# A selective-scan recurrence on one NeuronCore: outputs summed turned in PSUM, one of four input scalings on VectorE

## The reference

```python
u, res = silu(x @ W_in[:, :256]), (x @ W_in[:, 256:])
delta  = softplus(u @ W_delta + b_delta)          # 512 positions x 256 channels
Bm, Cm = u @ W_B, u @ W_C                         # 512 positions x 16 states
# over time, for each of 256 channels and 16 states:
h[t] = exp(delta[t] * A) * h[t-1] + delta[t] * B[t] * u[t]
y[t] = sum over the 16 states of h[t] * C[t]
out  = ((y + u * D_param) * silu(res)) @ W_out
```

## Time and profile before

| | us |
|---|---|
| median of 3 runs (lowest, highest) | 1144.26 (1143.19, 1144.58) |
| the profiled execution: its own time | 1145.62 |
| its span, first to last instruction | 1143.8 |
| TensorE busy in the span | 837.0 (73%) |
| VectorE busy | 816.1 (71%) |
| ScalarE busy | 700.0 (61%) |
| GpSimd busy | 292.4 (26%) |

### The profile page before, as it was taken

The page is one execution under the profiler, slowest core; times in us unless marked ns, Lnnn a source line. Parts: engine busy times, 40 slices in busy tenths (PEclk is TensorE's granted clock), DMA queues, the critical chain, the costliest instruction groups (busy, mean ns, idle before and its releaser), DMA issues. The chain is left out here.

```text
span 1143.8 us, 12084 instructions
## 1 busy us (share of the span) xinstructions
PE 837.0 (73%) x3574; PEld 505.8 (44%) x3576; DVE 816.1 (71%) x1651; ACT 700.0 (61%) x2225; POOL 292.4 (26%) x170
## 2 busy tenths in 40 slices
PE   2661285999977489998976137699996847998883
PEld 2450244555746334354445023455574633435432
DVE  2169745887555679998976873688845568999993
ACT  1411449995478385956851235999458828596591
POOL 0002103886356300000001110488635520000000
PEclk9865586999999899999996559699999979999997
DMA  8101002321000000000000001132100000000000
GB/s 229 38 0 33 0 8 61 93 93 47 1 1 1 1 1 1 0 1 0 1 19 0 0 1 37 42 96 95 32 1 1 1 0 1 1 1 1 1 1 19
DMA packets 26812, 27.37 MB, mean 24 GB/s; under 512 B 7172, under 2 KB 17146, under 8 KB 26746
## 3 DMA queue, kind: packets, MB, share of 16 engines
q1 hardware_dynamic: 24776, 24.63, 7.4%
q10 hardware_dynamic: 1970, 1.97, 0.6%
HBM read 25.28 MB, written 1.31 MB: 23 GB/s over the span
## 5 line engine op out<-in xcount | busy, mean ns | idle before, releaser
L1553 POOL TENSOR_TENSOR rs<-ve,minus_half 128x4 f32<-128x4 f32 (+1 forms) x56 | 89.3, 1596 | 647.6 <-DVE ve L1194 558.4
L943 PE MATMUL ps<-mem,ident 128*128 128x512 f32 x512 | 230.9, 600 | 31.1 <-DVE mem L1522 30.5
L1154 ACT ACTIVATE mem<-mem 128x32 f32<-128x32 f32 x1024 | 217.8, 309 | 0.0
L975 ACT ACTIVATE mem<-ps 128x512 f32<-128x512 f32 (+7 forms) x108 | 66.1, 612 | 205.1 <-PE ps L949 58.1
L1568 POOL TENSOR_TENSOR mem<-mem 128x1024 f32<-128x1024 f32 x64 | 150.8, 2359 | 116.6 <-DVE mem L1369 116.4
L1369 DVE TENSOR_TENSOR_SCAN mem<-mem,ps 128x1024 f32<-128x1024 f32 x64 | 145.9, 2285 | 45.3 <-PE ps L784 45.3
L1522 DVE SCALAR_TENSOR_TENSOR mem<-mem 128x1024 f32<-128x1024 f32 x128 | 159.3, 1279 | 15.3 <-ACT mem L1154 13.9
L943 PEld LDWEIGHTS ps<-mem,ident 128*128 128x128 f32 x512 | 94.1, 190 | 166.8 <-issue 92.4
L791 PE MATMUL ps<-mem,ident 128*128 128x512 f32 x256 | 121.9, 603 | 0.0
L1122 ACT ACTIVATE mem<-ps,mem,rs 128x77 f32<-128x77 f32 x256 | 101.9, 443 | 18.6 <-DVE mem L1425 18.6
L1514 DVE TENSOR_TENSOR mem<-mem 128x1024 f32<-128x1024 f32 x96 | 113.0, 1218 | 0.3
(11 more groups left out here) (220 smaller groups left out, 1229.6 us busy)
## 6 DMA issues: line engine op xcount, KB each, us to landing
mem<-bc_rows SPq DMA_DIRECT2D x64, 256.0 KB, 3.1
xin<-in_x_dram SPq DMA_DIRECT2D x4, 256.0 KB, 3.5
out_dram<-x SPq DMA_DIRECT2D x4, 256.0 KB, 2.3
mask<-in_mask_BxSxS_ik_dram SPq DMA_DIRECT2D x4, 154.0 KB, 3.8
mem<-n_L_ffn_expert_down_dram SPq DMA_DIRECT2D x1, 512.0 KB
mem<-in_L_xattn_Wo_dram SPq DMA_DIRECT2D x1, 512.0 KB
mem<-in_L_xattn_Wv_dram ACTq DMA_DIRECT2D x1, 512.0 KB
a_q<-in_L_xattn_Wq_dram SPq DMA_DIRECT2D x1, 512.0 KB, 4.8
```

What stands on the lines that cost most here:

```text
L943: mm = pe.matmul(ps[:, j, :], ident[:], WH[s][:, h % WB, j * 512:(j + 1) * 512], start=(h == 0), stop=(h == PH - 1), skip_group_check=True)
L1154: ins = nc.scalar.activation(SVA[s][:, n % 2, i * NK:(i + 1) * NK], sims[:, 1, h, :], ACT.Identity, bias=sims[:, 0, h, i:i + 1])
L1553: nc.gpsimd.tensor_tensor(RS[s][0:rows, i * n:(i + 1) * n], VE[s][0:rows, i * n:(i + 1) * n], minus_half[0:rows, 0:n], ALU.pow)\
```

## The change

Three edits, all in the scan:

1. **The sum.** The `HC` products are no longer added up as they lie. Each of the 8 blocks of 128x128 is transposed into banks 0 and 1 with accumulation over the states, so the sum stands there turned (time on the partitions). After the loop ScalarE copies it to SBUF (`YT`, 1024 columns) and TensorE transposes it back once, 8 transposes, into the same banks, where VectorE takes it as before.
2. **The scaling.** ScalarE makes three of the four blocks of `DZ`; VectorE makes the fourth, `own_product`: a `TENSOR_SCALAR` of 256 columns, SBUF to SBUF, float32. It is written into VectorE's queue one state ahead: own product n+1 of lane 0, of lane 1, then scan n of lane 0, of lane 1. TensorE waits for both parts of `DZ`.
3. **Semaphores.** `dz_own` is new, `ln_ready` is folded into `softplus_step`, and the counts follow.

```diff
 TensorE, loop:
                             yield (3.7, 4.0)[s] + n
                             w.next(G("dz_ready", s))
+                            w.next(G("dz_own", s))
...
                             w.next(G("hc_done", s))
-                            for j in range(DJ):
-                                mm = pe.matmul(ps[:, j, :], ident[:], HC[s][:, (n - 1) % 2, j, :],
-                                               start=(n == 1), stop=(n == NS), skip_group_check=True)
+                            for k in range(NB):
+                                for j in range(DJ):
+                                    at = k % 2 * DI + j * P
+                                    mm = pe.matmul(ps[:, k // 2, at:at + P],
+                                                   HC[s][:, (n - 1) % 2, j, k * P:(k + 1) * P], ident[:],
+                                                   start=(n == 1 and at == 0), stop=(n == NS and at == 3 * P),
+                                                   is_transpose=True, skip_group_check=True)
                             mm.then_inc(G("y_acc", s), 1)
+                    yield 4.9 + NS
+                    w.next(G("xT_ready", s))
+                    for j in range(DJ):
+                        for k in range(NB):
+                            mm = pe.transpose(ps[:, j, k * P:(k + 1) * P], YT[s][:, k, j * P:(j + 1) * P], ident[:])
+                    mm.then_inc(G("y_acc", s), 1)
 ScalarE:
-                        for k in range(NB):
+                        for k in range(NB - 1):
                             ins = nc.scalar.activation(DZ[s][:, n % 2, k, :], DUT[s][:, k, :], ACT.Identity,
                                                        scale=BT[s][:, k, n:n + 1])
                         ins.then_inc(G("dz_ready", s), 1)
+                    yield 4.85 + NS
+                    w.next(G("y_acc", s), NS)
+                    copy(YT[s][:].rearrange("p (a b) c -> p a (b c)", a=2), ps[:, 0:2, :], G("xT_ready", s))
 VectorE:
+                    def own_product(n):
+                        if n == 0:
+                            w.reach(G("xT_ready", s), XT_TURNS)
+                            w.next(G("bc_sb", s), 2)
+                        if n >= 2:
+                            w.reach(G("dbu_done", s), n - 1)
+                        nc.vector.tensor_scalar(DZ[s][:, n % 2, NB - 1, :], DUT[s][:, NB - 1, :],
+                                                BT[s][:, NB - 1, n:n + 1], None, ALU.mult)\
+                            .then_inc(G("dz_own", s), 1)
+
+                    yield 3.45
+                    own_product(0)
                     for n in range(NS):
+                        if n + 1 < NS:
+                            yield (4.05, 4.15)[s] + n
+                            own_product(n + 1)
                         yield 4.2 + n
...
                     yield 5 + NS
-                    w.next(G("y_acc", s), NS)
+                    w.next(G("y_acc", s), NS + 1)
```

More of the change, by code:

```diff
@@ L258, in decoder @@
             sm=(P, (2, 8), F32), rd=(P, (2, 8), F32))
+        _, YT = per_lane(front=(P, (10 * DJ * S,), F32), yT=(P, (NB, DI), F32))
         _, KW = per_lane(front=(P, (10 * DJ * S,), F32), kw=(P, (H, C), F32))
@@ L289, in decoder @@
         TURNS = dict(
-            x_loaded=16, ctx_loaded=16, mask_loaded=16, stored=16, x_ready=6, turned=18, xT_ready=8,
+            x_loaded=16, ctx_loaded=16, mask_loaded=16, stored=16, x_ready=6, turned=18, xT_ready=9,
             u_ready=6, conv0=2, v1_ready=1, y_ready=1, v3_ready=1, o_ready=4, var_ready=14, rstd_ready=14,
             s_ready=9, l_ready=9, p_ready=9, pT_ready=1, q_ready=5, qT_ready=5, h_ready=4, hpre_ready=4,
-            g_ready=8, silu_u=2, silu_r=2, d_ready=2, bc_ready=2, ln_ready=1, delta_ready=2, bc_sb=2,
-            bc_out=16, C_even=128, C_odd=128, dA_ready=16, dz_ready=16, dbu_done=16, scan_done=16,
-            hc_done=16, y_acc=16, yg_ready=1, k_ready=5, ksq_ready=2, kn_ready=1, kT_ready=1, v_ready=3,
+            g_ready=8, silu_u=2, silu_r=2, d_ready=2, bc_ready=2, delta_ready=2, bc_sb=2,
+            bc_out=16, C_even=128, C_odd=128, dA_ready=16, dz_ready=16, dz_own=16, dbu_done=16, scan_done=16,
+            hc_done=16, y_acc=17, yg_ready=1, k_ready=5, ksq_ready=2, kn_ready=1, kT_ready=1, v_ready=3,
             v_sb=3, qsq_ready=4, xr_ready=1, sim_ready=4, sim_sb=4, wh_ready=32, wh_used=32, z_ready=8,
             g_sb=4, hw_ready=4, hwT_ready=4, aq_ready=4, own_done=30, pn_ready=8, wT_ready=12, eo_ready=4,
-            eo_drained=4, asum_ready=8, softplus_step=3, kvar_ready=1, krstd_ready=1, m_sb=2, ssq_done=4,
+            eo_drained=4, asum_ready=8, softplus_step=4, kvar_ready=1, krstd_ready=1, m_sb=2, ssq_done=4,
             rd_ready=8, wT_turned=12, at_used=12)
@@ L1050, in scan @@
                     w.next(G("softplus_step", s))
-                    nc.scalar.activation(SPA[s][:], SPE[s][:], ACT.Ln, bias=1.0).then_inc(G("ln_ready", s), 1)
+                    nc.scalar.activation(SPA[s][:], SPE[s][:], ACT.Ln, bias=1.0).then_inc(G("softplus_step", s), 1)
                     for n in range(NS):
@@ L1355, in scan @@
                     w.next(G("own_done", s), DJ)
-                    w.next(G("ln_ready", s))
+                    w.next(G("softplus_step", s), 2)
                     w.link(nc.vector.tensor_tensor(DL[s][:], DL[s][:], SPA[s][:], ALU.add))
```

## The result

| | time, median of runs | lowest to highest | ratio, 95% interval |
|---|---|---|---|
| before | 1143.93 us (4) | 1143.19 to 1144.58 | |
| after | 1192.2 us (4) | 1190.84 to 1195.72 | 1.0419 (1.0394 to 1.0443) |

The change costs 48 us, 4.2%. The profiled execution of after took 1192.85 us with a span of 1191.1; before it was 1143.8.

A forecast was written before the change was run, and what follows sets the result against it. ScalarE was taken to set the pace, 5.64 us a period. Loop 23.0, start -0.4, end 1.25, last `HC`s 0.13 gave 24.0 a pass, 48 for two: 1145.6 to 1193.6, median 1.4 below, 1192; range 1123 to 1206.

The forecast's parts named there:

- ScalarE, TensorE, VectorE by themselves: In the loop, without waits: ScalarE's period falls from 5.64 to 4.84 us, TensorE leaves the bound, VectorE's is 4.91.
- Exclusion: In the loop VectorE's `own_product` cannot run beside GpSimd's `HC`; with a wait for each product, chance 0.70.
- The period: Loop, one state of both lanes: 7.32 us with waits, making the loop 106.8 against 83.8, +23.0 a pass.
- The end of the loop: From last `HC` to keys: 3.2 us instead of 1.96, with last sum, copy and transposes; +1.25 a pass.
- case C: Rival: transposes alone halve TensorE's clock, 1180 us, chance 0.04; with products waiting, only post-loop work costs, up to 1.8 a pass.
- The start: At the loop's start the first `DZ` comes one activation earlier: -0.4 us a pass.
- The last `HC`s: At the loop's end the last `HC`s are pushed by the one ahead: +0.13 us a pass.
- A: Rival: in the loop the fourth product runs freely, VectorE sets a period of 4.91, 1125 us; chance 0.13.
- B: Rival: products and `HC` exclude each other, but both products go as a pair in one gap; period 5.15, 1132; chance 0.08.
- D: Rival: gains and waits cancel in the loop, a product held about 0.35 each time; period 5.6, 1144 us; chance 0.05.

The follow-up runs named there:

- the separated order: Kernel after, with VectorE's queue changed to own product 0, scan 0, own product 1, scan 1; 1125.6 us against 1144.41, ratio 0.9832.
- accumulator run: Kernel after, with `own_product` also writing its row sum to an accumulator output that nobody reads; 1138.05 us against 1144.41, ratio 0.9935.
- the sum alone: Kernel after, but ScalarE makes all four `DZ` products and VectorE none; 1150.73 us, ratio 1.0049; run again for a profile, 1152.05, ratio 1.0074.
- the half `HC`: Kernel after, with GpSimd multiplying only the first channel group, 512 columns instead of 1024, and the sum taking it twice; 1147.57 us, ratio 1.0035.

## Why the prediction was right

It said 1192, and the median is 1192.2. The mechanism is the one it described; its steps are off by more than 0.2, in both directions.

- **ScalarE, TensorE, VectorE by themselves.** ScalarE's cover was real: in after it is busy for 71% of the loop, GpSimd stands for 2.43 a period (2.5 was said). A product that meets nobody takes 0.345 to 0.354 ahead of the loop and 0.327 in the loop of the separated order, where 0.348 was worked out; there it adds 0.24 to the queue (0.28 was said).
- **Exclusion**, the step with 0.70 on it. Shown, from three sides: the plain product is held (2.88 for two), the form with an accumulator at the same place is not (0.45 and 0.48), and the hold shrinks with the `HC` (2.47 to 1.38). "It must be using more than one way into SBUF" had been drawn from two speeds, and from unlike ones: 0.52 ns is what a further column costs, 1.3 a whole duration over its columns. Two sizes of `TENSOR_TENSOR` before give a further column 1.04 ns there ((1218 - 687)/512), so the factor is two and not two and a half. The accumulator run agrees with the inference (the form that isn't held is the slower one), but no run shows how many ways are in use.

```profile
L1514 DVE TENSOR_TENSOR mem<-mem 128x1024 f32<-128x1024 f32 x96 | 113.0, 1218 | 0.3
...
L1292 DVE TENSOR_TENSOR r<-x 128x512 f32<-128x512 f32 x4 | 2.7, 687 | 0.1
```

- **The period.** 7.32 was said, 7.17 measured. The order of events was the one described: own 0 gets in at the first `HC`'s end, `HC` 1 gets in before own 1, own 1 ends behind it. Two sizes were off. The two `HC`s were to end at 4.82 and end at 4.75. Of this the wait of `HC` 1 for own 0 was nearly right: two at a time with no product between them take 4.66 in the same trace (four take 9.29, at the loop's end), so it lost 0.08 where 0.10 was said; but 2.36 + 2.36 left out that two rows in a row overlap by 0.05. And own 1 ends 0.15 after `HC` 1, not 0.20. That makes the loop 104.7 instead of 106.8: 2.1 too much.
- **The end of the loop.** 3.2 was said from the last `HC` to the keys, 4.3 measured: 1.1 too little. Where the clock stays full, after the separated order and with the accumulator, it is 3.19 each. The prediction had this under its case C, "half clock costs only the work after the loop, up to 1.8 us a pass", and gave it no place in the likeliest sum; it belongs there. That part of C came true in after and in the sum alone; that the clock would sink for the whole loop did not: the mean in the loop is 0.89 in both.
- **The start.** From the first `dA` to the first scan it takes 9.95 before and 9.55 after, in both passes: the 0.4 that was said. The first scan of the program stands 0.8 earlier because the first `dA` already does so by 0.4, ahead of the edited stage (from the timelines of before and of after):

```profile
177.79 1.33 ACT L1060 ACTIVATE mem<-mem,m_A 128x511 f32<-128x511 f32 x2
```

```profile
177.39 1.33 ACT L1072 ACTIVATE mem<-mem,m_A 128x511 f32<-128x511 f32 x2
```

- **The last `HC`s** end 0.04 earlier (0.13 later was said).

From the first `dA` to the keys a pass costs 22.8 more (102.98 and 125.81; 22.9 in the second), where the prediction's sum was 24.0. For two that is 45.7 against 48. The span grew by 47.3 and the median by 48.3, so 1.5 to 2.6 us lie outside the two scans, where the prediction had nothing. Its loop was too long, its end and what it had outside too short, and these cancelled. That the median is met to 0.2 us is luck; that the two passes are met to 2.3 us of 48 is not.

Of the rivals, A (a free product, 1125) was a true price for a thing that didn't happen in this kernel: the separated order has a period of 4.88 where A had 4.91, and 1125.6. B (the pair in one gap) fell: GpSimd got in between the two products in all 28 pairs of after (the first 0.49 to 0.51, the second 2.45 to 2.47), and in all 28 with the half `HC`, where it came after 0.90 of idling and the first product had met nobody (0.32 to 0.33). D would have asked for a hold of 0.35, and it is 2.1.

What isn't settled: 2 to 3 us of the turned sum's cost by itself, and some us outside the two scans in every comparison (among the traces that were read the first scan starts anywhere from 183.9 to 189.9, and not in the order of the edits). Nor why the clock sinks, in the loop and after it, in after and in the sum alone but stays full with the separated order, the accumulator and the half `HC`, though all have nothing but these transposes on TensorE. Its busy time doesn't tell them apart (below); its longest pause in a period is 3.06 us in after and 1.93 in the sum alone, and 1.80, 1.04 and 0.8 in the other three, but no run changed the pauses by themselves.

## What to carry to other kernels

Before work is moved to an idle VectorE, look at what the two engines share, not only at busy shares: here a plain float32 `TENSOR_SCALAR` from SBUF to SBUF and a GpSimd `TENSOR_TENSOR` took turns, and a product of 0.33 us stood for up to 2.47. Two such products back to back let GpSimd in between, so that the second waits for a whole instruction of it and everything queued behind it waits as well; put one at a time where GpSimd's next instruction is released by what VectorE has just finished, or take a form that is not held, here the one with an accumulator output. And a relief for an engine that doesn't set the period is worth nothing until the one that does is relieved, while its costs outside the loop are due at once.

## What the runs showed of the hardware that was not expected

- An excluded product costs the other side almost nothing: two `HC`s with a product let in between take 4.73 to 4.76, two without one 4.66 in the same trace; in the separated order each `HC` takes 2.40 in place of 2.36.
- The exclusion does not cover the whole of a row. In the separated order a product of 0.33 overlaps the last 0.12 of one `HC`'s row and the first 0.16 of the next, and is not lengthened. The 0.15 by which a held product outlasts the `HC` is less than its 0.33, too.
- Loops with nothing on TensorE but float32 transposes had a mean granted clock of 0.89 in two kernels (TensorE busy for 47.36 of 60 in the sum alone, 38.50 in after) and of 1.00 in the separated order (39.70 of 50). The two gave half clock, 1.2 in place of 2.4 GHz, to the last sum and the turning back of the first two.
